# Adaptive-mix FFN with a top-2 LoRA on one core: full-height second lora product for two tiles, an earlier row operation, and a split first piece of W

## The reference, cut to what matters

```
h   = gelu(gelu(cond @ W0 + b0) @ W1 + b1)            # 32 rows, exact gelu
att = softmax(h @ W2 + b2)                            # [32, 8]
agg_w = einsum('bk,koi->boi', att, weight)            # 64x64 per batch entry
agg_b = att @ bias_k
y   = agg_w @ x + agg_b                               # x: [32, 64, 1024] fp32, per batch entry
p   = softmax(y @ gate_W.T); top 2 of 8 experts, weights renormalised
out = x + y @ W_base.T + ((y @ A) * w_dense * 2.0) @ B   # A, B: 8 experts of rank 8
```

## Time and profile before

| what | value |
|---|---|
| median of three runs | 257.17 us |
| time of the profiled execution | 257.24 us |
| its span in the trace | 255.5 us |
| PE busy | 250.4 us, 98% |
| PE weight loads busy | 243.0 us, 95% |
| DVE busy | 127.6 us, 50% |
| ACT busy | 87.7 us, 34% |
| GpSimd busy | 9.5 us, 4% |
| data moved | 35.27 MB |

### The profile page before, as it was taken

The page is one execution under the profiler, slowest core; times in us unless marked ns, Lnnn a source line. Parts: engine busy times, 40 slices in busy tenths (PEclk is TensorE's granted clock), DMA queues, the critical chain, the costliest instruction groups (busy, mean ns, idle before and its releaser), DMA issues.

```text
span 255.5 us, 4274 instructions
## 1 busy us (share of the span) xinstructions
PE 250.4 (98%) x1456; PEld 243.0 (95%) x1456; DVE 127.6 (50%) x400; ACT 87.7 (34%) x205; POOL 9.5 (4%) x27
## 2 busy tenths in 40 slices
PE   8999999999999999999999999999999999999993
PEld 5899989898999999999999999999999999999992
DVE  2998643374845554345355444445545434535342
ACT  4677675816141231413132141324123141313120
POOL 6000042000000000000000000000000000000000
PEclk9999999999999999999999999999999999999999
DMA  6999868040551606051240706033060705122022
GB/s 176 406 403 316 346 176 305 17 164 3 225 185 48 201 1 246 1 176 70 86 160 0 246 0 227 19 117 129 38 208 0 244 3 174 75 87 77 3 82 82
DMA packets 10921, 35.27 MB, mean 138 GB/s; under 512 B 1264, under 2 KB 1824, under 8 KB 10912
## 3 DMA queue, kind: packets, MB, share of 16 engines
q1 hardware_dynamic: 10912, 35.15, 39.5%
HBM read 26.73 MB, written 8.39 MB: 137 GB/s over the span
## 4 chain that ended last, share of the span: by engine, by line
PE 98%; DVE 1%; issue 0%; POOL 0%; DVEq 0%; POOLq 0%
PE z_ps L764 25%; PE z_ps L765 25%; PE z_ps L766 25%; PE o_ps L783 3%; PE o_ps L789 3%; PE o_ps L788 3%; PE o_ps L780 3%; PE o_ps L778 3%; PE t_ps L843 2%; PE s_ps L813 1%; PE o_ps L764 1%; PE o_ps L765 1%; PE o_ps L766 1%; PE t_ps L804 0%; PE o_ps L892 0%; DVE z_lo L539 0%
## 5 line engine op out<-in xcount | busy, mean ns | idle before, releaser
L764 PE MATMUL z_ps<-w_hi,xt_hi 128*128 128x366 f32 (+1 forms) x376 | 125.8, 335 | 0.0
L765 PE MATMUL z_ps<-w_lo,xt_hi 128*128 128x366 f32 (+1 forms) x376 | 124.2, 330 | 0.0
L766 PE MATMUL z_ps<-w_hi,xt_lo 128*128 128x366 f32 (+1 forms) x376 | 124.0, 330 | 0.0
L764 PEld LDWEIGHTS z_ps<-w_hi,xt_hi 128*128 128x128 f32 x376 | 70.8, 188 | 0.7 <-issue 0.6
L765 PEld LDWEIGHTS z_ps<-w_lo,xt_hi 128*128 128x128 f32 x376 | 71.0, 189 | 0.2 <-issue 0.2
L766 PEld LDWEIGHTS z_ps<-w_hi,xt_lo 128*128 128x128 f32 x376 | 70.7, 188 | 0.0
L539 DVE TENSOR_TENSOR z_lo<-z_ps,z_hi 128x366 fp32r<-128x366 f32 (+1 forms) x47 | 25.3, 538 | 82.1 <-ACT z_hi L397 82.0
L397 ACT ACTIVATE z_hi<-z_ps 128x366 fp32r<-128x366 f32 (+1 forms) x47 | 22.4, 476 | 123.6 <-PE z_ps L766 123.6
L554 DVE TENSOR_TENSOR xt_lo<-xt_raw,xt_hi 128x1024 fp32r<-128x1024 f32 x14 | 17.2, 1225 | 17.7 <-ACT xt_hi L387 17.7
L617 DVE TENSOR_TENSOR out_sb<-o_ps,x_nat 128x366 f32<-128x366 f32 (+1 forms) x44 | 19.9, 505 | 4.5 <-PE o_ps L789 3.8
L778 PE MATMUL o_ps<-z_hi,blk_hi 128*128 128x366 f32 (+1 forms) x48 | 16.2, 338 | 0.0
(11 more groups left out here) (111 smaller groups left out, 178.8 us busy)
## 6 DMA issues: line engine op xcount, KB each, us to landing
x_nat<-x_in SPq DMA_DIRECT2D x16, 512.0 KB, 4.7
out<-out_sb SPq DMA_DIRECT2D x15, 512.0 KB, 3.0
xt_raw<-xt_in SPq DMA_DIRECT2D x14, 512.0 KB, 5.2
w_nat<-wn_in SPq DMA_DIRECT2D x8, 512.0 KB, 4.7
w_raw<-wext_in SPq DMA_DIRECT2D x8, 366.0 KB, 8.9
w_raw<-wext_in SPq DMA_DIRECT2D x4, 364.0 KB, 5.8
xt_raw<-xt_in SPq DMA_DIRECT2D x4, 256.0 KB, 5.4
par<-small_in SPq DMA_DIRECT2D x1, 576.0 KB, 7.2
```

Of the source, the lines that this page charges most:

```text
L764: nc.tensor.matmul(dst, hi, w_cols(w_hi, g, k), start=(k == 0), stop=False)
L765: nc.tensor.matmul(dst, hi, w_cols(w_lo, g, k), start=False, stop=False)
L766: last = nc.tensor.matmul(dst, lo, w_cols(w_hi, g, k), start=False, stop=(k == KC - 1))
```

## The change

It has three parts.

1. `lora_b` rows 64 to 127 are zeroed once by GpSimd, and line 789 multiplies all 128 rows for tiles 0 and 1 too. Since `b_lo` rows 64 to 127 are now read by these products, `sum_copy(0)`, which overwrites rows 64, 65 and 96 of it, waits until tile 1's lora products are done (`main_done`), and moves on ACT from before `x_high` to behind `z_high(t, 0)` of tile 2.
2. On DVE `row_low(0)` moves from behind to ahead of the second z split and the gating of tile 2.
3. Piece 0 of W is loaded as two DMAs of one chunk each; DVE splits chunk by chunk; PE starts with chunk 0 once that is split. The four dummy matmuls before it are gone.

```diff
@@ semaphores
-        w_loaded = [sem(f"w_loaded{n}") for n in range(PIECES)]
+        w_loaded = [None] + [sem(f"w_loaded{n}") for n in range(1, PIECES)]
+        w0_loaded = [sem("w0_loaded_chunk0"), sem("w0_loaded_chunk1")]
+        w0_lo_ready = sem("w0_lo_ready")
@@ SP
             load_x01(0, 0)
-            load_w(0)
+            for k in range(PC):
+                sp.dma_start(w_cols(w_raw, 0, k), w_cols(wext, 0, k)).then_inc(w0_loaded[k], 16)
             load_x01(1, 0)
...
-            sp.wait_ge(row_zeroed, 1)
+            sp.wait_ge(row_zeroed, 2)
@@ GpSimd
+            nc.gpsimd.memset(lora_b[ROW_HI:P, :].bitcast(U32), 0).then_inc(row_zeroed, 1)
+            pool.wait_ge(row_zeroed, 1)
             nc.gpsimd.memset(bias_row[ROW_HI:P, :, :], 0.0).then_inc(row_zeroed, 1)
-            pool.wait_ge(row_zeroed, 1)
+            pool.wait_ge(row_zeroed, 2)
@@ ACT
             def sum_copy(h):
                 act.wait_ge(sum_mm, h + 1)
-                act.wait_ge(b_lo_ready, 1)
+                act.wait_ge(main_done, 2 * G)
@@ ACT, step
                 lora_copy(t - 1, biased=not sums)
-                if sums:
-                    sum_copy(0)
                 if not last:
                     x_high(j + parity, 1 - parity)
                 z_high(t, 0)
+                if sums:
+                    sum_copy(0)
                 block_high(t, parity)
@@ DVE
             def w_low(n):
-                dve.wait_ge(w0_hi_ready if n == 0 else w_hi_ready, max(n, 1))
+                dve.wait_ge(w_hi_ready, n)
@@ DVE, step
                 add_out(j - 1 + parity, 1 - parity, first=early)
+                if early:
+                    row_low(0)
                 if last:
                     gating(t)
                     z_low(t, 1)
                 else:
                     z_low(t, 1)
                     gating(t)
-                if early:
-                    row_low(0)
@@ DVE, start
             x0_high(0)
             x_low(0, 0)
-            dve.wait_ge(w_loaded[0], 16)
-            nc.vector.tensor_copy(piece(w_hi, 0), piece(w_raw, 0)).then_inc(w0_hi_ready, 1)
-            w_low(0)
+            for k in range(PC):
+                dve.wait_ge(w0_loaded[k], 16)
+                nc.vector.tensor_copy(w_cols(w_hi, 0, k), w_cols(w_raw, 0, k)).then_inc(w0_hi_ready, 1)
+                dve.wait_ge(w0_hi_ready, k + 1)
+                nc.vector.tensor_tensor(w_cols(w_lo, 0, k), w_cols(w_raw, 0, k), w_cols(w_hi, 0, k).bitcast(F32),
+                                        ALU.subtract).then_inc(w0_lo_ready if k < PC - 1 else w_lo_ready, 1)
@@ PE
-            def lora_pair(dst, cols, biased, start=False):
-                rows = slice(0, P if biased else ER)
+            def lora_pair(dst, cols, start=False):
                 nc.tensor.matmul(dst, lora_t[:, :], b_hi[:, cols], start=start, stop=False, skip_group_check=True)
-                return nc.tensor.matmul(dst, lora_b[rows, :], b_lo[rows, cols], start=False, stop=not start,
+                return nc.tensor.matmul(dst, lora_b[:, :], b_lo[:, cols], start=False, stop=not start,
                                         skip_group_check=True)
@@ PE, start
-            warm(4)
-
...
-            first_z(0, 0)
+            pe.wait_ge(x01_lo_ready, 1)
+            pe.wait_ge(w0_lo_ready, 1)
+            z_group(0, 0, 0, chunks=range(1), bank_free=True)
+            pe.wait_ge(w_lo_ready, 1)
+            z_group(0, 0, 0, chunks=range(1, PC), bank_free=True)
             first_z(1, 0)
             first_z(0, 1)
...
             pe.wait_ge(b_lo_ready, 1)
+            pe.wait_ge(row_zeroed, 1)
             lora_groups(0, copies=2)
```

More of the change, by code:

```diff
@@ L798, in lora_groups @@
                     dst = o_ps[g][:, SKIP[g]:SKIP[g] + OUTN[g]]
-                    lora_pair(dst, cols, copies is None).then_inc(main_done, 1)
+                    lora_pair(dst, cols).then_inc(main_done, 1)
             def transpose_lora(t):
@@ L948, in _ @@
             dst = o_ps[G - 1][:, 0:WIDTH[G - 1]]
-            lora_pair(dst, slice(OUT0[G - 1], D), True, start=True)
+            lora_pair(dst, slice(OUT0[G - 1], D), start=True)
             o_group(t, 1, G - 1, start=False)
```

## The result

Twelve runs of the changed kernel had a median of 256.6 us (256.04 to 260.04), twelve of the kernel before beside them 258.06: a ratio of 0.994, with a 95% interval of 0.9916 to 0.9963. A second set gave 0.9961 (0.9941 to 0.9981). (The run at 260.04 is a slow one; ratios here are of fast runs alone.) The change takes 1.5 us off by the first set and 1.0 by the second, where 2.4 were forecast. The time of 256.6 is 1.8 us above the forecast of 254.8 and outside its range. Half of that is the shortfall of 0.9 us. The other half is the starting point: the three runs that the forecast stood on had a median of 257.17, and larger sets of the same kernel give 257.5 to 258.1.

A forecast was written before the change was run, and what follows sets the result against it. PE, 98% of the last-ending chain, was taken as the bound. 257.24 - 1.16 - 1.15 - 0.22 + 0.1 (tile 1's wait) + 0.1 (second DMA) = 254.9, less 0.07 for the median: 254.8 us, range 254.3 to 255.9.

The forecast's parts named there:

- Tile 1's wait: PE before tile 1's lora products: the eighth row sum's block of W would land sooner; cost taken 0.1 us.
- The bound of 1.16: Most that PE could lose at tile 1, in us, if the eighth row sum's block of W came no sooner.
- the rival at 0.08: Tile 1's gain is eaten by the eighth row sum's load of W; time around 255.8 us, chance 0.08.
- The copies on ACT: Moved sum_copy(0), three copies of 0.59 us before tile 2's block_high: about 0.3 us of cover, no cost.
- the later clock: At the start, without dummies, PE's clock rises later; PE about 0.65 us late at att_rep, 255.5 us, chance 0.22.
- the head start: PE's first z matmuls: three matmuls ahead of before, worth nothing by itself, absorbing 0.5 us of slow clock.
- the second DMA: Loading piece 0 in two DMAs might delay piece 1 of W and att_rep; cost taken 0.1 us, bounds 0 and 0.44.
- the terms: Gains of parts 1 and 2: 1.16 us at tile 0's lora products, 1.15 at tile 1's, 0.22 at the row sums.

The follow-up runs named there:

- rows64_all: The kernel before with 64 rows in the second lora product of every tile, bias of tiles 2 to 15 left out; 272.87 us against 257.74.
- after_wn7_early: The changed kernel with the eighth block of W_base loaded early into a free part of w_raw; ratio to before 0.9904.
- after_sums_behind: The changed kernel with the last two row sums on ACT moved out of z_high's way, sum_copy(0) behind tile 2's block_high; ratio to before 0.9895.
- after_warm4: The changed kernel with the four dummy matmuls put back ahead of the first z matmul; ratio to before 0.996.
- lora_only: The kernel before with parts 1 and 2 of the change, keeping the old start (one DMA for piece 0, four dummies); ratio to before 0.9949.
- best_new_start_warm: The changed kernel with the last two row sums and sum_copy(0) moved later on ACT and the four dummies kept; 254.12 us, ratio to before 0.9866.
- again_after: The changed kernel measured once more, nothing altered; ratio to before 0.9961, its profiled execution 258.64 us.

## Why the prediction was right and wrong

**Part 1: right.** 1.10 and 1.11 us stood where 2.28 and 2.27 had been, and `rows64_all` shows the price over 14 more tiles. The sentence of the Trainium skill ("TensorE: Matmul & The Clock Gate", Part 3, the mechanism), that loads overlap a running matmul only when their row groups differ, doesn't hold here: 128-row and 96-row loads run ahead of the running matmul, with 0.0 us idle before 48 of them. The same section also lets loads into the background weight buffer run ahead; that fits these two heights, but no trace here shows the buffer, and it gives no reason why 64 rows don't.

**Tile 1's wait: the step that failed.** The forecast said: "That product comes 1.16 us sooner, so the load is issued about 1.1 us sooner and lands, at the same 4.5 us, near 43.4", and took 0.1 us. The first half held; the load didn't move, because the fifth row sum has a second condition, its own transfer, that was level with the ratio before. And "the same 4.5 us" didn't hold: over the eight profiled executions with the change's order of row sums the eighth block took 3.61 to 6.06 us. PE's wait for z_high is 0.61 - 0.17 = 0.44 us in the profiled execution, and 0.94 to 2.75 in the seven others; PE then waits for z_low as well. In all, from the second z matmul behind tile 0's lora products to the start of tile 1's, PE took 46.99 - 36.55 = 10.44 us before and 47.79 - 36.67 = 11.12 after, 0.68 more. The seven others took 1.18 to 3.20 more, and the middle of the eight is 1.47, where the sum had 0.1. The bound of 1.16 was no bound: once PE no longer set the pace here, it carried the whole scatter of a chain of two transfers. This was the rival at 0.08, and it deserved most of the chance. That it is the main loss is shown twice over, by `after_wn7_early` and `after_sums_behind`. Why the eighth block's transfer varies by over two microseconds, while the fifth's stayed within 4.11 to 4.64, was not found.

**The copies on ACT: right.** No wait for tile 2's block product appeared, and with z_high no longer late the later place of `sum_copy(0)` cost nothing either.

**Part 2: right**, 0.22 us, and shown by its undoing.

**Part 3: right that it brings nothing by itself; the later clock did come.** In ten of the seventeen profiled executions the attention product started 3.84 to 3.86 us behind the start of ACT's split of piece 1, whatever PE did before: 8.21 to 12.06 before, 9.53 to 13.38 after. In the other seven PE came last, by 0.07 to 0.91 us. In the profiled pair the head start only made PE wait longer there. That split came between 8.07 and 9.53 us in kernels with two DMAs and between 8.11 and 8.80 with one, so the +1.32 us of the profiled pair is mostly the spread of executions. The means are 8.60 and 8.34; that leaves up to 0.3 us for the second DMA, where 0.1 was taken, but with this spread it isn't shown. The rival of the clock (0.22) happened: of seven profiled executions with the four dummies the pitch fell at 9.2 to 9.6 us in four, before the first z matmul in two and at 11.0 in one; in ten without them it fell at 10.3 to 13.1 (in one of these, `after_sums_behind`, the first two starts at 7.4 us were 0.17 apart, and then the granted clock fell to 0.5 until 11.4). It was given 0.65 us at the attention product; PE was up to 0.9 late there. Why the dummies bring nothing inside the change (`after_warm4`) isn't shown. That tile 1's wait takes up the delay is a guess with a gap: the second row sum, behind which the chain of two transfers starts, began 21.7 us after the attention product in every execution, so a late attention product delays the chain too. Yet in the eight executions with that chain the third block product came at 46.49 to 47.80 and didn't follow the attention product, at 11.93 to 13.38. The forecast priced each rival alone, and not what one does to the other.

**The sum.** Parts 1 and 2 bring 2.9 us by the trace of `after_sums_behind` where the terms say 2.53. Of the other 0.3, 0.12 is PE's old wait for z_low ahead of tile 1's lora products, which is gone there too; the rest isn't accounted for. The middle of the eight executions lost 1.6 us against that trace at tile 1, and 2.9 - 1.6 = 1.3 is what `lora_only` measured. With both losses away, `best_new_start_warm` stands at 0.9866, 3.4 us under before; with them the change keeps 1.0 to 1.5. The rest of the miss in microseconds, the low median of the three runs that the forecast started from, was bad luck.

## What to carry to other kernels

A wait that the profile doesn't show may be one that another wait just covers. Before booking a gain on the bound engine in full, follow each queue that is to move with it back to every condition of its head, the transfers above all. A gain in front of a chain of transfers can be lost, in part or whole, until a load is taken out of that chain (another buffer) or the chain out of the way (its consumer moved behind the urgent work), and either is worth trying together with the change. Don't drop fillers ahead of the first real work without measuring; here they were worth about 0.3% once nothing hid them. And don't put half-height stationary loads among full ones.

## What the runs showed of the hardware

- Heights of a stationary load among 128-row ones: 128 and 96 rows, no idle time before them; 64 rows, 0.18 to 0.19 us before each of 48 and about 1.1 us for six matmuls. Other heights were not run.
- In `again_after` PE idle for 2.59 us was followed by a pitch of 0.30 us from 48.25 to 51.2 and a granted clock of 0.50; in the seven executions with 2.08 us and less idle at the same place the pitch stayed at 0.17.
- One and the same 512 KB load took 3.61 to 6.06 us from one execution to another.
